# Two rows per layer norm instruction, and a float32 product as three fp32r passes, in a four-stage graph and expert network on one core

## The chip, the cores and the metric

The kernel runs on one core of one Trainium2 chip. Its five engines work side by side, each on its own queue of instructions in program order: PE (TensorE, matrix products), DVE (VectorE), ACT (ScalarE), POOL (GpSimd) and SP (SyncE, which here only issues DMAs). They are tied together by semaphores that the kernel sets and awaits itself: no scheduler moves anything. The metric is the device time of one execution in microseconds.

## The reference

There are 128 graphs of 128 nodes with 128 features. Four residual blocks follow one another, each on a layer norm of what stands before it; `_layernorm` is over the 128 features of one node:

```
def _layernorm(x, axis=-1, eps=1e-05):
    m = jnp.mean(x, axis=axis, keepdims=True)
    v = jnp.var(x, axis=axis, keepdims=True)
    return (x - m) / jnp.sqrt(v + eps)
...
    x = x + _L0_gnn_ref(_layernorm(x, axis=-1), adj, ...)       # 5 groups of nodes, two graph convolutions
    x = x + _L0_ffn_ref(_layernorm(x, axis=-1), ...)            # 8 experts, best 2 of each node
    x = x + _L1_gnn_ref(_layernorm(x, axis=-1), adj, nodemask, ...)
    x = x + _L1_ffn_ref(_layernorm(x, axis=-1), ...)            # shared MLP + 4 experts, best 2
```

The shared MLP of the last block, whose second product is changed:

```
        def _shared_mlp(x, W1, b1, W2, b2, W3, b3):
            h = jax.nn.relu(x @ W1 + b1)
            h = jax.nn.relu(h @ W2 + b2)
            return h @ W3 + b3
```

## The kernel before

All of `x` stays in the chip's memory as `xtok`: 128 partitions (the node), 128 graphs, 128 features. So the "row" of one layer norm is 128 contiguous float32 of one partition, and two graphs' rows of the same node lie 512 bytes apart. Layer norm is made of steps on several engines: DVE takes `bn_stats` of one graph (six numbers per node: for the even and for the odd features a count, a mean and a sum of squared deviations) and `bn_aggr`, which joins the two halves to mean and variance; DVE adds the epsilon (`pre`), POOL raises it to the power -1/2 (`root`), DVE makes the bias (`nb`), and ACT applies scale and bias (`xn`, `xs`, `xl`).

The program runs four stages one after another.

1. **First stage (0 to about 240 us).** Turns `t` = 0 to 27, written out. In turns 0 to 15 (`first`) one batch of grouped nodes gets its layer norm (four `bn_stats`, L650, four `bn_aggr`, L654) and starts its graph convolutions. In turns 9 to 24 (`second`) eight graphs get the result added (L645) and the statistics of the second layer norm: eight `bn_stats` (helper `stats`, L630, in groups of 2, 3, 3) and eight `bn_aggr` (helper `averages`, L635, in groups of 4 and 4), then `gpre` (L727), POOL's `groot` (L415) and `gnb` (L763). `search` finds the two best experts. Turns 9 to 15 carry `first` and `second` both.
2. **Sorting** of the nodes by expert (to about 300 us).
3. **Expert stage** (to about 817 us): 71 tiles of 512 nodes. Nothing in it is changed.
4. **Last stage (about 818 us to the end).** Four graphs are one batch; there are 32 batches and 36 turns `j`. One turn works on five batches in different phases: `complete` (batch j: gather both experts' rows, add them to `xtok`), `norm` (j-1: third layer norm), `aggregate` (j-2: graph product, then the fourth layer norm), `hidden` (j-3: the last block's first products and its router) and `finish` (j-4: the rest, and the output).

In the last stage the order on each queue is that of the code. On DVE one turn is, with the lines that matter: addition of the identity to the adjacency `at` (L1654); `stats(j-1, 0)`: four `bn_stats` of the third layer norm (L1636); `x4l` (L1663), the low part of `x4t`; `averages` of the same (L1644); the router's first step (L1669); `variance` (L1649), which lets POOL start the root; `cwd` (L1682), which waits for PE's transpose `p_ta` (L1529); bias and update (L1690 to L1702); `stats(j-2, 1)` and `averages` of the fourth layer norm (L1636, L1644), `variance` (L1649); router steps; `rc` (L1731, L1739), which PE's last products (L1553) wait for; router steps, and among them `nb[1]` (L1755), which waits for POOL's second root; the output sum `outx` (L1780); `cws` (L1786 to L1789); and `choice(0)` and `choice(1)` (L1629): the gathered rows of batch j times their probabilities added to `xtok`, four instructions each, with the copy `idx` between (L1797).

POOL has in each turn four indirect gathers, root 0, four indirect gathers, root 1, in this order (`body`, L1372 to L1390). Root 0 waits for the third layer norm's variance, root 1 for the fourth's.

Of the shared MLP, PE multiplies by `sW1` in `up(c, E1)` (L1557) as three passes in fp32r: weights and data are each split into a high part that fp32r holds and a low part, and hi x hi, lo x hi and hi x lo are summed in PSUM. The second product (L1509, in the helper `product`, L1469) takes float32 operands: `ws[:, P:2*P]` times `hs[0]`, which ACT's `relu` (L1460, at L1405) wrote at the end of the turn before. Its result is read by ACT's next `relu` into `hs[1]` (L1432).

Of the kernel before, what the change touches and what calls it, by code (L numbers as in the profile page):

```python
# [16 lines left out]
F32 = mybir.dt.float32  # L17
F16 = mybir.dt.float16
F32R = mybir.dt.float32r
# [6 lines left out]
P = 128  # L26
# [75 lines left out]
def build(nc, x_tok, x_grp, a_grp, w_grp, fus, wg, bg, w_exp, a_t, w_gcn, b_gcn, mask_t,  # L102
# [8 lines left out]
    with top:  # L111
# [90 lines left out]
        with ExitStack() as ctx:  # L202
# [19 lines left out]
            st = [alloc(ctx, f"st{p}", [P, R, 6]) for p in range(2)]  # L222
            mv = [alloc(ctx, f"mv{p}", [P, R, 2]) for p in range(2)]
# [19 lines left out]
            gst = alloc(ctx, "gst", [P, RG, 6])  # L243
            gmv = [alloc(ctx, f"gmv{p}", [P, RG, 2]) for p in range(2)]
# [72 lines left out]
            with nc.Block() as block:  # L317
# [264 lines left out]
                def _(dve):  # L582
# [30 lines left out]
                    for t in TURNS:  # L613
# [14 lines left out]
                        def stats(ks):  # L628
                            for k in ks:
                                last = nc.vector.bn_stats(gst[:, k, :], xtok[:, RG * b + k, :])  # L630
                            return last

                        def averages(ks):
                            for k in ks:
                                last = nc.vector.bn_aggr(gmv[u][:, k, :], gst[:, k, :])  # L635
                            return last
# [10 lines left out]
                        if first:  # L647
                            dve.wait_ge(loaded[p], 32 * (t // 2) + 32)
                            for k in range(R):
                                last = nc.vector.bn_stats(st[p][:, k, :], xg[p][:, k, :])  # L650
                            last.then_inc(stat_s, 1)
                            dve.wait_ge(stat_s, t + 1)
                            for k in range(R):
                                last = nc.vector.bn_aggr(mv[p][:, k, :], st[p][:, k, :])  # L654
                            last.then_inc(mv_s, 1)
                            dve.wait_ge(mv_s, t + 1)
                            nc.vector.tensor_scalar(pre[p][:, 0:R], mv[p][:, :, 1], 1e-5, None, ALU.add)
# [13 lines left out]
                        if second:  # L671
                            dve.wait_ge(x1_ready, b + 1)
                            stats(range(2))
# [3 lines left out]
                        if second:  # L677
                            stats(range(2, 5))
# [3 lines left out]
                        if second:  # L682
                            stats(range(5, RG)).then_inc(gstat_s, 1)
# [11 lines left out]
                        if first:  # L695
                            dve.wait_ge(dinv_s, 4 * t + 1)
                            dve.wait_ge(root_done, t + 1)
                            nc.vector.tensor_tensor(dinv[t % GA][:, :], nz[p][:, :], root[p][:, R:2 * R], ALU.mult)\
                              .then_inc(dinv_s, 1)
                            dve.wait_ge(dinv_s, 4 * t + 2)  # L700
                            nc.vector.tensor_tensor(dsc[p][:, :], dinv[t % GA][:, :], root[p][:, 0:R], ALU.mult)\
                              .then_inc(dinv_s, 1)
                            dve.wait_ge(dinv_s, 4 * t + 3)
                            nc.vector.scalar_tensor_tensor(xsb[p][:, :], mv[p][:, :, 0], -1.0, dsc[p][:, :],
                                                           ALU.mult, ALU.mult).then_inc(xsb_ready, 1)
                            dve.sem_inc(dinv_s, 1)
# [5 lines left out]
                        if second:  # L712
                            dve.wait_ge(gstat_s, b + 1)
                            averages(range(R))
# [3 lines left out]
                        if second:  # L718
                            averages(range(R, RG)).then_inc(gmv_s, 1)
                        if search:  # L720
                            m0 = mask[0][:, RG * c:RG * c + RG, :]
                            m1 = mask[1][:, RG * c:RG * c + RG, :]
                            after(4)
                            step(same(m0, wd, tv[2]))
                        if second:
                            dve.wait_ge(gmv_s, b + 1)
                            nc.vector.tensor_scalar(gpre[u][:, :], gmv[u][:, :, 1], 1e-5, None, ALU.add)\  # L727
                              .then_inc(gpre_ready, 1)
# [32 lines left out]
                        if second:  # L761
                            dve.wait_ge(groot_done, b + 1)
                            nc.vector.scalar_tensor_tensor(gnb[u][:, :], gmv[u][:, :, 0], -1.0, groot[u][:, :],  # L763
                                                           ALU.mult, ALU.mult).then_inc(gnb_ready, 1)
# [480 lines left out]
        with ExitStack() as ctx:  # L1245
# [15 lines left out]
            st = [alloc(ctx, f"st_l{k}", [P, R, 6]) for k in range(2)]  # L1261
            mv = [alloc(ctx, f"mv_l{k}", [P, R, 2]) for k in range(2)]
# [54 lines left out]
            x4l_ready = sem("l_x4l_ready")  # L1317
            w1_s = sem("l_w1_s")
# [18 lines left out]
            with nc.Block() as block:  # L1337
# [60 lines left out]
                def _(act):  # L1398
# [17 lines left out]
                    def body(i, p, complete, norm, aggregate, hidden, finish):  # L1416
# [42 lines left out]
                        if hidden:  # L1459
                            relu(c, 4, hs[0][:, :], bs[:, 0:1])  # L1460

# [3 lines left out]
                def _(pe):  # L1465
# [26 lines left out]
                    def body(i, p, complete, norm, aggregate, hidden, finish):  # L1492
# [74 lines left out]
                def _(dve):  # L1567
# [29 lines left out]
                    nc.vector.tensor_copy(w1h[:, 0:E1, :], w1[:, :, :])  # L1597
                    nc.vector.tensor_copy(w1h[:, E1, :], ws[:, 0:P]).then_inc(w1_s, 1)
                    dve.wait_ge(w1_s, 1)
                    nc.vector.tensor_tensor(w1l[:, 0:E1, :], w1[:, :, :], w1h[:, 0:E1, :].bitcast(F32), ALU.subtract)  # L1600
                    nc.vector.tensor_tensor(w1l[:, E1, :], ws[:, 0:P], w1h[:, E1, :].bitcast(F32), ALU.subtract)\
# [14 lines left out]
                    def body(i, p, complete, norm, aggregate, hidden, finish):  # L1616
# [18 lines left out]
                        def stats(n, k, r):  # L1635
                            ins = nc.vector.bn_stats(st[k][:, r, :], row(n, r))  # L1636
                            if r == R - 1:
                                ins.then_inc(ln[k], 1)
# [12 lines left out]

                        if norm:
# [6 lines left out]
                            for r in range(R):  # L1659
                                stats(j - 1, 0, r)  # L1660
# [4 lines left out]
                        if norm:  # L1665
                            averages(j - 1, 0)
# [20 lines left out]
                        if norm:  # L1687
# [5 lines left out]
                            nc.vector.scalar_tensor_tensor(nbm[:, :], mv[0][:, :, 0], -1.0, rd[:, :],  # L1693
# [10 lines left out]
                        if aggregate:  # L1704
                            dve.wait_ge(x3_ready, j - 1)
                            dve.sem_inc(passed, 1)
                            for r in range(R):
                                stats(b, 1, r)
# [3 lines left out]
                        if aggregate:  # L1712
                            averages(b, 1)
# [39 lines left out]
                        if aggregate:  # L1753
                            dve.wait_ge(root_done[1], j - 1)
                            nc.vector.scalar_tensor_tensor(nb[1][:, :], mv[1][:, :, 0], -1.0, root[1][:, :],  # L1755
# [117 lines left out]
```

## Time and profile before

| | us |
|---|---|
| median of 3 runs | 1334.93 (1333.78 to 1335.29) |
| the profiled execution's own time | 1336.69 |
| its span, first to last instruction | 1334.8 |
| PE busy | 1193.2 (89%) |
| DVE busy | 1137.0 (85%) |
| ACT busy | 997.9 (75%) |
| POOL busy | 843.4 (63%) |
| mean granted TensorE clock | 0.937 |

Busy times are sums of durations, and a duration of an engine that pipelines its work reaches past the start of the next instruction. So the time that an instruction costs its queue is the distance from its start to the next one's start, which the timeline view shows. Idle time in front of an instruction stands in square brackets with what ended it, if it is long enough to be listed.

### The profile page before, as it was taken

The page shows a single profiled execution, that of the slowest core. Times are in us where ns is not written, and L with a number is a line of the kernel's source. Part 1 is how long each engine was busy: PE and PEld are TensorE (multiplying, and loading weights), DVE is VectorE, ACT ScalarE, POOL GpSimd, SP SyncE. Part 2 cuts the span into 40 slices and gives each one's busy share as a digit, 9 for nine tenths or more (in the row PEclk, how much of TensorE's full clock was granted, in tenths as well). Part 3 has the DMA queues.
Part 4 walks back from the last instruction along what each step waited for, and adds up shares of the span by engine and source line. Part 5 has one row for each costly group of instructions (what it writes and reads, how often), then busy time and mean ns, then how long its engine had stood idle before and what let it go on. Part 6 is the DMA issues. An engine that isn't in the chain of part 4 may idle for free. (4 is left out here: it accounts for less than half of the span.)

```text
span 1334.8 us, 21838 instructions
## 1 busy us (share of the span) xinstructions
PE 1193.2 (89%) x6288; PEld 870.6 (65%) x6288; DVE 1137.0 (85%) x4033; ACT 997.9 (75%) x1947; POOL 843.4 (63%) x781
## 2 busy tenths in 40 slices
PE   5889988364999999999999993499999999999998
PEld 4767757253777777777777772366666666666665
DVE  4778998897899998999999996589898988989885
ACT  3457666493999999999999993477777777777774
POOL 3345555675777777777777763676666666667630
PEclk9999975576999999999999997599999999999999
DMA  5578764400222332322222262123222322222210
GB/s 183 200 234 265 210 184 137 169 1 19 69 80 78 78 78 78 80 79 80 79 78 79 77 77 62 54 62 85 65 70 69 84 67 70 76 76 68 68 48 24
DMA packets 137642, 124.89 MB, mean 94 GB/s; under 512 B 15630, under 2 KB 117106, under 8 KB 136371
## 3 DMA queue, kind: packets, MB, share of 16 engines
q1 hardware_dynamic: 119219, 88.06, 21.4%
q0 software_dynamic: 18304, 35.44, 11.8%
q8 instruction: 51, 0.84, 0.3%
q14 instruction: 68, 0.56, 0.1%
HBM read 83.78 MB, written 39.67 MB: 92 GB/s over the span
## 5 line engine op out<-in xcount | busy, mean ns | idle before, releaser
L1069 POOL DMA_INDIRECT exg<-xln_scratch,eidx x284 | 315.2, 1110 | 124.3 <-issue 69.3
L1362 POOL DMA_INDIRECT yg<-expert_rows_scratch,idx x256 | 253.4, 990 | 95.2 <-issue 72.5
L1208 DVE TENSOR_TENSOR ehl<-ehr,ehh 128x512 fp32r<-128x512 f32 x284 | 194.7, 686 | 28.7 <-ACT ehh L1093 28.5
L1090 ACT ACTIVATE ehr<-p_eh,bc 128x512 f32<-128x512 f32 x284 | 195.9, 690 | 25.1 <-PE p_eh L1128 17.0
L1093 ACT ACTIVATE ehh<-ehr 128x512 fp32r<-128x512 f32 x284 | 179.6, 633 | 9.0
L1369 POOL TENSOR_TENSOR root_l<-pre_l,mhalf 128x4 f32<-128x4 f32 x64 | 66.6, 1041 | 96.9 <-DVE pre_l L1649 96.2
L1126 PE MATMUL p_ey<-ehh,wh 128*128 128x512 f32 x284 | 124.8, 439 | 1.0 <-DVE ehl L1208 0.8
L1126 PE MATMUL p_eh<-exh,wh 128*128 128x512 f32 x284 | 124.0, 437 | 1.5 <-DVE exl L1203 1.5
L1128 PE MATMUL p_eh<-exh,wl 128*128 128x512 f32 x284 | 112.6, 396 | 0.0
L1127 PE MATMUL p_eh<-exl,wh 128*128 128x512 f32 x284 | 112.2, 395 | 0.0
L1128 PE MATMUL p_ey<-ehh,wl 128*128 128x512 f32 x284 | 111.9, 394 | 0.0
L1127 PE MATMUL p_ey<-ehl,wh 128*128 128x512 f32 x284 | 111.5, 393 | 0.0
L1405 ACT ACTIVATE he<-p_lh,be 128x512 f32<-128x512 f32 x128 | 87.8, 687 | 21.9 <-PE p_lh L1479 21.9
L1190 DVE TENSOR_TENSOR wl<-wall,wh 128x512 fp32r<-128x512 f32 x142 | 98.5, 693 | 4.9
L1629 DVE SCALAR_TENSOR_TENSOR xtok<-yg,prob,xtok 128x128 f32<-128x128 f32 x256 | 73.0, 346 | 19.3 <-DMA yg<-expert_rows_scratch,idx 16.7
L1126 PEld LDWEIGHTS p_ey<-ehh,wh 128*128 128x128 f32 x284 | 53.1, 187 | 47.6 <-DVE ehl L1208 40.7
L1475 PE MATMUL p_lh<-x4h,w1h 128*128 128x512 f32 x160 | 77.2, 483 | 1.4 <-ACT he L1405 1.3
L1411 ACT ACTIVATE xn<-xtok,nb,rd 128x128 f32<-128x128 f32 x128 | 52.8, 482 | 28.2 <-DVE nb L1702 28.1
L1553 PEld LDWEIGHTS p_out<-w,rc 128*128 128x128 f32 x512 | 59.6, 191 | 18.0 <-DVE rc L1731 17.9
L1553 PE MATMUL p_out<-w,rc 128*128 128x128 f32 x512 | 65.4, 281 | 5.1 <-DVE rc L1731 2.6
L911 PE MATMUL p_id<-hh,lc 128*128 128x284 f16 x224 | 40.5, 349 | 32.4 <-DVE hh L978 32.4
L1469 PE MATMUL p_lh<-he,w 128*64 128x512 f32 x256 | 68.8, 617 | 0.0
(228 smaller groups left out, 3152.8 us busy)
## 6 DMA issues: line engine op xcount, KB each, us to landing
expert_rows_scratch<-eyo SPq DMA_DIRECT2D x71, 256.0 KB, 2.3
xtok<-in_x_tok SPq DMA_DIRECT2D x8, 1024.0 KB, 6.8
an<-in_a_t SPq DMA_DIRECT2D x16, 512.0 KB, 4.5
xln_scratch<-xl SPq DMA_DIRECT2D x16, 512.0 KB, 4.3
at<-in_a_t SPq DMA_DIRECT2D x32, 256.0 KB, 3.0
out<-outx SPq DMA_DIRECT2D x32, 256.0 KB, 2.6
wj<-in_w_grp SPq DMA_DIRECT2D x16, 321.0 KB, 4.5
exg<-xln_scratch,eidx POOLq DMA_INDIRECT x284
```

The lines of the kernel that those rows point to most:

```text
L1069: pool.indirect_dma_start(out=xg[p][:, k, :], out_offset=None, in_=xln_d, in_offset=bass.IndirectOffsetOnAxis(ap=idx[p][:, k:k + 1], axis=0))\
L1090: nc.scalar.activation(hr[c % 2][:, :], p_h[c][:, :], ACT.Relu, bias=bc[p][:, c:c + 1])\
L1093: nc.scalar.activation(hh[:, c, :], hr[c % 2][:, :], ACT.Copy).then_inc(hh_ready, 1)
L1126: nc.tensor.matmul(dst, w_hi, a_hi, start=start, stop=False)
L1127: nc.tensor.matmul(dst, w_hi, a_lo, start=False, stop=False)
L1128: return nc.tensor.matmul(dst, w_lo, a_hi, start=False, stop=stop)
L1190: nc.vector.tensor_tensor(wl[p][:, cols], w[:, cols], wh[p][:, cols].bitcast(F32), ALU.subtract).then_inc(ready, 1)
L1208: nc.vector.tensor_tensor(hl[:, c, :], hr[c % 2][:, :], hh[:, c, :].bitcast(F32), ALU.subtract)\
L1362: pool.indirect_dma_start(out=yg[p][:, c, k, :], out_offset=None, in_=y_d, in_offset=bass.IndirectOffsetOnAxis(ap=idx[p][:, c, k:k + 1], a ...
L1405: nc.scalar.activation(dst, p_h[u % 2][:, :], ACT.Relu, bias=bias).then_inc(h_ready, 1)
L1475: nc.tensor.matmul(dst, w1h[:, e, :], x4h[:, :], start=True, stop=False)
L1553: last = nc.tensor.matmul(p_out[:, k, :], rc[u][:, k * P:(k + 1) * P], w3[:, u, :], start=False, stop=(u == 1 and k == R - 1))
```

## The change

**Statistics of two rows at once.** A new helper, `two_rows`, gives `bn_stats` two graphs' rows interleaved (feature 0 of the first, feature 0 of the second, feature 1 of the first, and so on). The instruction keeps even and odd elements apart, so each graph's count, mean and sum of squared deviations come out in three numbers. `bn_aggr` is left out everywhere, with its waits; the variance is the third number over 128, and this factor goes into the instruction that adds the epsilon. All three places use it: the two layer norms of the first stage and the two of the last.

**Three passes.** The product with `sW2` is made as `up` makes the first: weights split once into `s2h` and `s2l` at the start of the stage; each turn ACT copies `hs[0]` to `hsh` (fp32r) right after its `relu`, and DVE subtracts to get `hsl`, placed between `choice(0)` and the copy of `idx` (in the turns up to 7, and where no batch is completed, ahead of `choice(0)`).

```
+        def two_rows(dst, src):
+            return nc.vector.bn_stats(dst.rearrange("p r s -> p (r s)"), src.rearrange("p r d -> p d r"))
...
-            st = [alloc(ctx, f"st_l{k}", [P, R, 6]) for k in range(2)]
-            mv = [alloc(ctx, f"mv_l{k}", [P, R, 2]) for k in range(2)]
+            st = [alloc(ctx, f"st_l{k}", [P, R, 3]) for k in range(2)]
...
                             relu(c, 4, hs[0][:, :], bs[:, 0:1])
+                            act.wait_ge(h_ready, 8 * c + 7)
+                            nc.scalar.activation(hsh[:, :], hs[0][:, :], ACT.Copy).then_inc(hsh_ready, 1)
...
                             second(c - 1, 6, 1)
-                            product(c - 1, 7, [(p_h[1][:, :], ws[:, P:2 * P], hs[0][:, :])])
+                            pe.wait_ge(h_ready, 8 * c)
+                            pe.wait_ge(hsh_ready, c)
+                            nc.tensor.matmul(p_h[1][:, :], s2h[:, :], hsh[:, :], start=True, stop=False)
+                            nc.tensor.matmul(p_h[1][:, :], s2l[:, :], hsh[:, :], start=False, stop=False)
+                            pe.wait_ge(hsl_ready, c)
+                            nc.tensor.matmul(p_h[1][:, :], s2h[:, :], hsl[:, :], start=False, stop=True)\
+                              .then_inc(h_done, 1)
...
-                        def averages(n, k):
-                            dve.wait_ge(ln[k], 2 * n + 1)
-                            dve.sem_inc(passed, 1)
-                            for r in range(R):
-                                last = nc.vector.bn_aggr(mv[k][:, r, :], st[k][:, r, :])
+                        def stats(n, k):
+                            for r in range(0, R, 2):
+                                last = two_rows(st[k][:, r:r + 2, :], xtok[:, R * n + r:R * n + r + 2, :])
                             last.then_inc(ln[k], 1)
 
                         def variance(n, k):
-                            dve.wait_ge(ln[k], 2 * n + 2)
-                            nc.vector.tensor_scalar(pre[k][:, :], mv[k][:, :, 1], 1e-5, None, ALU.add)\
+                            dve.wait_ge(ln[k], n + 1)
+                            nc.vector.tensor_scalar(pre[k][:, :], st[k][:, :, 2], 1.0 / D, 1e-5, ALU.mult, ALU.add)\
                               .then_inc(pre_ready[k], 1)
...
+                        filling = isinstance(j, int) and j < 8
+
+                        def rest():
+                            dve.wait_ge(hsh_ready, j - 2)
+                            nc.vector.tensor_tensor(hsl[:, :], hs[0][:, :], hsh[:, :].bitcast(F32), ALU.subtract)\
+                              .then_inc(hsl_ready, 1)
+
+                        if hidden and (filling or not complete):
+                            rest()
                         if complete:
                             dve.wait_ge(gathered[p], 64 * i + 128)
                             dve.sem_inc(passed, 1)
                             for r in range(R):
                                 choice(0, r)
+                            if hidden and not filling:
+                                rest()
```

In the first stage, `second`'s eight `bn_stats` become four (in groups of 1, 1 and 2 where they were 2, 3 and 3), and `first`'s four become two. Two setup instructions on DVE make `s2h` and `s2l`.

How the order moves on DVE in a middle turn of the last stage, from `choice(0)` to the third layer norm's variance (`yg` are gathered rows, `st_l` statistics, `mv_l` mean and variance, `sm` router scores, `pre_l` variance plus epsilon). Before:

```order
L1629 SCALAR_TENSOR_TENSOR xtok<-yg,prob,xtok 128x128 x4
L1797 COPY idx<-pos_i 128x8
L1629 SCALAR_TENSOR_TENSOR xtok<-yg,prob,xtok 128x128 x4
L1654 TENSOR_TENSOR at<-at,cf 128x512
L1636 BN_STATS st_l<-xtok 128x6 x4
L1663 TENSOR_TENSOR x4l<-x4t,x4h 128x512
L1644 BN_AGGR mv_l<-st_l 128x2 x4
L1669 TENSOR_TENSOR sm<-p_llg,gbs 128x16
L1649 TENSOR_SCALAR pre_l<-mv_l 128x4
```

The same stretch of DVE's queue in the changed kernel:

```order
L1630 SCALAR_TENSOR_TENSOR xtok<-yg,prob,xtok 128x128 x4
L1783 TENSOR_TENSOR hsl<-hs,hsh 128x512
L1796 COPY idx<-pos_i 128x8
L1630 SCALAR_TENSOR_TENSOR xtok<-yg,prob,xtok 128x128 x4
L1648 TENSOR_TENSOR at<-at,cf 128x512
L151 BN_STATS st_l<-xtok 128x6 x2
L1656 TENSOR_TENSOR x4l<-x4t,x4h 128x512
L1660 TENSOR_TENSOR sm<-p_llg,gbs 128x16
L1643 TENSOR_SCALAR pre_l<-st_l 128x4
```

`hsl` (128x512) has come in, two of four `bn_stats` and all four `bn_aggr` have gone. On ACT, from the end of one turn into the next (`hs`, `rp`: results of the `relu`s; `x4t`, `x4h`: the last block's input, whole and high part; `agt`: the graph product), before:

```order
L1411 ACTIVATE xn<-xtok,nb,root_l 128x128 x4
L1405 ACTIVATE hs<-p_lh,bs 128x512
L1405 ACTIVATE rp<-p_lh,be 128x512
L1424 ACTIVATE x4t<-p_tb 128x512
L1426 ACTIVATE x4h<-x4t 128x512
L1429 ACTIVATE agt<-p_ta 128x512
```

And in the changed kernel:

```order
L1402 ACTIVATE xn<-xtok,nb,root_l 128x128 x4
L1396 ACTIVATE hs<-p_lh,bs 128x512
L1453 ACTIVATE hsh<-hs 128x512
L1396 ACTIVATE rp<-p_lh,be 128x512
L1415 ACTIVATE x4t<-p_tb 128x512
L1417 ACTIVATE x4h<-x4t 128x512
L1420 ACTIVATE agt<-p_ta 128x512
```

`hsh` stands between the `relu` that makes `hs` and all that PE awaits from ACT at the start of the next turn.

## Rows read from the trace of the kernel before

**Rows 1.** Busy time by stretch: stretch, total, busy by engine, PEclk, DMA share, GB/s.

```profile
112.00:160.00 48.00, 46.49 (x315) 37.25 (x313) 45.88 (x236) 35.25 (x76) 27.77 (x16) 0.96 0.82 247
1000.00:1100.00 100.00, 98.00 (x553) 66.03 (x553) 89.67 (x438) 76.87 (x177) 67.10 (x68) 1.00 0.27 73
```

**Rows 2.** Chain that ended last, one turn of the last stage: start us, us, what.

```profile
897.31 1.06 POOL root_l L1369
...
900.99 1.14 DVE xtok L1629 x4
902.28 1.14 DVE xtok L1629 x4
...
903.94 0.86 DVE st_l L1636 x4
...
905.31 0.37 DVE mv_l L1644 x4
905.97 1.03 POOL root_l L1369
...
912.00 1.05 POOL root_l L1369
```

**Rows 3.** Timeline of DVE, one turn: start us, us, engine, line, operation, [idle before].

```profile
1051.41 0.86 DVE L1636 BATCH_NORM_STATS2 st_l<-xtok 128x6 f32<-128x128 f32 x4
1052.19 0.67 DVE L1663 TENSOR_TENSOR x4l<-x4t,x4h 128x512 fp32r<-128x512 f32 x1
1052.78 0.37 DVE L1644 BATCH_NORM_AGGREGATE mv_l<-st_l 128x2 f32<-128x6 f32 x4
1053.07 0.14 DVE L1669 TENSOR_TENSOR sm<-p_llg,gbs 128x16 f32<-128x16 f32 x1
...
1054.38 0.68 DVE L1682 TENSOR_TENSOR cwd<-p_ta,own 32x512 fp32r<-32x512 f32 x1 [0.72 <-PE p_ta L1529]
```

**Rows 4.** Waits from 900 to 1300 us: total us, times, longest us.

```profile
POOL root_l L1369 <- DVE pre_l L1649: 74.4, 28, 7.5
...
DVE cwd L1682 <- PE p_ta L1529: 12.3, 27, 0.7
...
DVE nb L1755 <- POOL root_l L1369: 7.7, 22, 0.6
```

**Rows 5.** DVE's groups by line: count, busy us, mean ns, idle before.

```profile
L953 DVE TENSOR_TENSOR posf<-p_rank,base_r 128x512 f32<-128x512 f32 x2 | 2.2, 1079 | 0.6 <-PE p_rank L903 0.6
...
L1581 DVE TENSOR_REDUCE selp<-selraw 32x256 fp32r<-32x1024 f32 x1 | 1.9, 1873 | 0.0
...
L1583 DVE TENSOR_REDUCE own<-selraw 32x4 f32<-32x1024 f32 x1 | 1.2, 1197 | 0.0
```

**Rows 6.** Timeline of PE, the same turn.

```profile
1050.63 1.12 PE L1469 MATMUL p_lh<-hs,ws 128*128 128x512 f32 x2
1051.59 0.95 PE L1515 MATMUL p_llg<-gws,x4t 128*128 128x4 f32 x8
...
1060.89 0.47 PE L1475 MATMUL p_lh<-x4h,w1h 128*128 128x512 f32 x1
...
1061.76 1.08 PE L1469 MATMUL p_lh<-he,w 128*64 128x512 f32 x4
```

**Rows 7.** Timeline of ACT, the same turn.

```profile
1049.52 0.63 ACT L1426 ACTIVATE x4h<-x4t 128x512 fp32r<-128x512 f32 x1
...
1051.79 0.69 ACT L1405 ACTIVATE hs<-p_lh,bs 128x512 f32<-128x512 f32 x1 [0.35 <-PE p_lh L1469]
1053.66 1.15 ACT L1437 ACTIVATE gr<-p_tb,dm 128x128 f32<-128x128 f32 x4 [1.18 <-PE p_tb L1521]
```

**Rows 8.** Timeline of the first stage, an early turn.

```profile
56.22 0.95 PE L521 MATMUL p_thin<-ones,ag 128*128 128x1 f32 x8
...
57.05 0.17 DVE L657 TENSOR_SCALAR pre<-mv 128x4 f32<-128x4 f32 x1
...
57.20 0.16 DVE L659 TENSOR_SCALAR nz<-p_thin 128x4 f32<-128x4 f32 x1
```

**Rows 9.** Timeline of DVE, first stage, a late turn.

```profile
202.97 0.17 DVE L763 SCALAR_TENSOR_TENSOR gnb<-gmv,groot 128x8 f32<-128x8 f32 x1 [0.25 <-POOL groot L415]
...
207.33 0.17 DVE L727 TENSOR_SCALAR gpre<-gmv 128x8 f32<-128x8 f32 x1
...
209.33 0.17 DVE L763 SCALAR_TENSOR_TENSOR gnb<-gmv,groot 128x8 f32<-128x8 f32 x1 [0.19 <-POOL groot L415]
```

More of the change, by code:

```diff
@@ L221, in build @@
             wb = alloc(ctx, "wb", [P, NGB])
-            st = [alloc(ctx, f"st{p}", [P, R, 6]) for p in range(2)]
-            mv = [alloc(ctx, f"mv{p}", [P, R, 2]) for p in range(2)]
+            st = [alloc(ctx, f"st{p}", [P, R, 3]) for p in range(2)]
             pre = [alloc(ctx, f"pre{p}", [P, 2 * R]) for p in range(2)]
@@ L242, in build @@
             tv = [alloc(ctx, f"tv{k}", [P, RG]) for k in range(3)]
-            gst = alloc(ctx, "gst", [P, RG, 6])
-            gmv = [alloc(ctx, f"gmv{p}", [P, RG, 2]) for p in range(2)]
+            gst = [alloc(ctx, f"gst{p}", [P, RG, 3]) for p in range(2)]
             gpre = [alloc(ctx, f"gpre{p}", [P, RG]) for p in range(2)]
@@ L629, in stats @@
                             for k in ks:
[L630 to L635, printed above, removed]
+                                last = two_rows(gst[u][:, k:k + 2, :], xtok[:, RG * b + k:RG * b + k + 2, :])
                             return last
@@ L648, in _ @@
                             dve.wait_ge(loaded[p], 32 * (t // 2) + 32)
-                            for k in range(R):
-                                last = nc.vector.bn_stats(st[p][:, k, :], xg[p][:, k, :])
+                            for k in range(0, R, 2):
+                                last = two_rows(st[p][:, k:k + 2, :], xg[p][:, k:k + 2, :])
                             last.then_inc(stat_s, 1)
                             dve.wait_ge(stat_s, t + 1)
[L653 to L657, printed above, removed]
+                            nc.vector.tensor_scalar(pre[p][:, 0:R], st[p][:, :, 2], 1.0 / D, 1e-5, ALU.mult, ALU.add)
                             dve.wait_ge(deg_done, t + 1)
@@ L672, in _ @@
                             dve.wait_ge(x1_ready, b + 1)
-                            stats(range(2))
+                            stats((0,))
                         if search:
@@ L677, in _ @@
                         if second:
-                            stats(range(2, 5))
+                            stats((2,))
                         if search:
@@ L682, in _ @@
                         if second:
-                            stats(range(5, RG)).then_inc(gstat_s, 1)
+                            stats((4, 6)).then_inc(gstat_s, 1)
                         if search:
@@ L711, in _ @@
                                                     ALU.mult).then_inc(zs_ready, 1)
-                        if second:
-                            dve.wait_ge(gstat_s, b + 1)
-                            averages(range(R))
                         if search:
@@ L725, in _ @@
                         if second:
-                            dve.wait_ge(gmv_s, b + 1)
-                            nc.vector.tensor_scalar(gpre[u][:, :], gmv[u][:, :, 1], 1e-5, None, ALU.add)\
+                            dve.wait_ge(gstat_s, b + 1)
+                            nc.vector.tensor_scalar(gpre[u][:, :], gst[u][:, :, 2], 1.0 / D, 1e-5, ALU.mult, ALU.add)\
                               .then_inc(gpre_ready, 1)
@@ L762, in _ @@
                             dve.wait_ge(groot_done, b + 1)
-                            nc.vector.scalar_tensor_tensor(gnb[u][:, :], gmv[u][:, :, 0], -1.0, groot[u][:, :],
+                            nc.vector.scalar_tensor_tensor(gnb[u][:, :], gst[u][:, :, 1], -1.0, groot[u][:, :],
                                                            ALU.mult, ALU.mult).then_inc(gnb_ready, 1)
@@ L1317, in build @@
             x4l_ready = sem("l_x4l_ready")
+            s2h = alloc(ctx, "s2h", [P, P], F32R)
+            s2l = alloc(ctx, "s2l", [P, P], F32R)
+            hsh = alloc(ctx, "hsh", [P, W], F32R)
+            hsl = alloc(ctx, "hsl", [P, W], F32R)
+            hsh_ready = sem("l_hsh_ready")
+            hsl_ready = sem("l_hsl_ready")
             w1_s = sem("l_w1_s")
@@ L1597, in _ @@
                     nc.vector.tensor_copy(w1h[:, 0:E1, :], w1[:, :, :])
+                    nc.vector.tensor_copy(s2h[:, :], ws[:, P:2 * P])
                     nc.vector.tensor_copy(w1h[:, E1, :], ws[:, 0:P]).then_inc(w1_s, 1)
@@ L1600, in _ @@
                     nc.vector.tensor_tensor(w1l[:, 0:E1, :], w1[:, :, :], w1h[:, 0:E1, :].bitcast(F32), ALU.subtract)
+                    nc.vector.tensor_tensor(s2l[:, :], ws[:, P:2 * P], s2h[:, :].bitcast(F32), ALU.subtract)
                     nc.vector.tensor_tensor(w1l[:, E1, :], ws[:, 0:P], w1h[:, E1, :].bitcast(F32), ALU.subtract)\
@@ L1658, in body @@
                             dve.sem_inc(passed, 1)
-                            for r in range(R):
-                                stats(j - 1, 0, r)
+                            stats(j - 1, 0)
                         if hidden:
@@ L1706, in body @@
                             dve.sem_inc(passed, 1)
-                            for r in range(R):
-                                stats(b, 1, r)
+                            stats(b, 1)
                         if hidden:
@@ L1754, in body @@
                             dve.wait_ge(root_done[1], j - 1)
-                            nc.vector.scalar_tensor_tensor(nb[1][:, :], mv[1][:, :, 0], -1.0, root[1][:, :],
+                            nc.vector.scalar_tensor_tensor(nb[1][:, :], st[1][:, :, 1], -1.0, root[1][:, :],
                                                            ALU.mult, ALU.mult).then_inc(nb_ready[1], 1)
```

15 lines of the change are left out of this document (2 added, 13 removed).

## The prediction, before the changed kernel ran

> **What bounds the kernel now.** I read the busy time by stretch first [rows 1]. In the last stage PE looks like the bound, 98 us of 100, DVE is at 90, ACT at 77, POOL at 67. But busy time counts pipelined durations past the next start, so it does not tell which engine is waited for. The chain that ended last does [rows 2]: between 860 and 960 us it holds no PE at all. It runs in a ring of DVE and POOL: POOL's second root of a turn (897.31) lets DVE make `nb[1]`; DVE goes on without a gap through the router, the output sum, both `choice` groups, the adjacency, `bn_stats`, `x4l`, `bn_aggr` and the variance; POOL's first root (905.97) waits for that, is followed by four gathers, and only then comes the second root (912.00). Once round is 912.00 - 897.31 = 14.69 us: 8.66 from the second root to the first, 6.03 from the first to the second. The waits say the same from both ends [rows 4]: POOL waits 74.4 us for the variance in 28 waits, 2.7 us each, and DVE waits for POOL's second root in 22 turns of 27, 7.7 us in all. So what DVE does between `nb[1]` and the third layer norm's variance costs its full length, and what it does in the other half, from the variance to `nb[1]`, has slack: 0.72 us ahead of `cwd` [rows 3] and some 0.3 us ahead of `nb[1]`. PE is close behind, since it takes part in a second ring over `cwd` and `rc`.
>
> In the first stage PE and DVE are both near full from 112 to 160 us, 46.5 and 45.9 us of 48 [rows 1].
>
> **What `hsl` costs in the ring.** It is a float32 subtraction of 128x512 into fp32r, as `x4l` is: 52.19 to 52.78, 0.59 us of the queue [rows 3]. It stands between `choice(0)` and `idx`, inside the ring half that has no gap. Its whole length is paid: +0.59 us a turn. Queued behind it are `choice(1)` and the variance, for which POOL waits. It hides nowhere: POOL's later four gathers come after root 0.
>
> **What the statistics give in the ring.** Four `bn_stats` take 51.41 to 52.19, 0.78 us, and four `bn_aggr` 52.78 to 53.07, 0.29 us [rows 3]; 1.07 go. Two two-row instructions come. The trace has none, so I bound one. Below: if it took elements at the rate of a contiguous one, its queue time is that of one `bn_stats`, 0.195 us, plus 128 more elements. The rate is that of the 1024 contiguous elements of L1583, (1197 - 130) / 1024 = 1.04 ns (130 ns being about the shortest duration of DVE, that of the small L1669) [rows 3, 5]: 0.195 + 0.133 = 0.33 us. Strided: the two-row instruction reads its elements 512 bytes apart, back and forth. The nearest row is L1581, which reduces the very data of L1583, but with steps of 1024 bytes from element to element: 1873 ns where the contiguous reading takes 1197 [rows 5], (1873 - 130) / 1024 = 1.70 ns. L953 writes in steps of 32 bytes and takes 1079 ns for 512 elements, while `x4l`, as large and contiguous, takes 670 [rows 3, 5]: the same kind of price. At 1.70 ns a two-row instruction is 256 x 1.70 = 0.435, plus the 0.06 that `bn_stats` has beside its 128 elements: 0.50 us, dearer than the 0.39 of the pair that it replaces. Upper end: alternating steps at twice the contiguous time, 0.60 us; no row excludes it. I take 0.50, by L1581, and keep 0.33 and 0.60.
>
> The Trainium skill has a rule on this, in "SBUF — State Buffer", "Door 1: The DMA port swizzle": memory lines are 16 bytes, and an access that crosses to another line pays, so only strides up to four float32 are free. Every element of a two-row read crosses. By that rule, and L1581 agrees with 1.63 times the time, the change loses in the ring. The other page, "VectorE: DVE Perf Modes", "Mode 1× (REGULAR) — the baseline", says of the plain mode that odd strides all work at one result per cycle. By that, the lower end would hold, which is the first rival; L1581 speaks against it.
>
> The ring then changes by +0.59 + 2 x 0.50 - 1.07 = +0.52 us a turn (contiguous +0.18, twice +0.72). It closes in the turns that have `hidden`, a batch to complete and gathers to issue, j = 3 to 30, less one that awaits a gather anyway: 27. So +14.0 us (+4.9; +19.4).
>
> **The other half of the ring, PE and ACT.** The fourth layer norm's statistics lie between `cwd` and `rc`: 1.00 for 1.07 us, hidden in the slack. PE's product takes 50.63 to 51.59, 0.96 us; three fp32r passes took 60.89 to 61.76, 0.87 us, where the next group begins [rows 6]. That is -0.1 us a turn on an engine that the ring does not wait for: nothing. It counts in the last four turns only, with the shorter statistics, -0.5 us in all. `hsh` costs ACT as much as `x4h`, 0.63 us. ACT stands idle 0.35 us before `hs[1]` and 1.18 before `gr` in that turn, 1.53 together, both waiting for PE [rows 7], so it is absorbed; were that cover gone, PE would be late by at most 0.6. `hsl` is ready at about 1050.2, and PE wants it half a microsecond after 1050.63 at the earliest. The setup of `s2h` and `s2l` stands in DVE's queue ahead of a wait for the first gathers: nothing.
>
> **First stage.** Turns 0 to 8: the variance is ready at 57.05 + 0.17, but the step after it, L659, starts at 57.20, about when PE's sums L521 end (56.22 + 0.95 = 57.17) [rows 8]. An earlier variance gives nothing. Turns 9 to 15 (7 turns): six pairs at +0.11 are +0.66, twelve `bn_aggr` at 0.29 per four are -0.87, a semaphore wait less -0.1: -0.31 us each, on an engine that is full: -2.2 us. Turns 16 to 24: DVE's path `gnb` to `gpre` (202.97 to 207.33) and POOL's root back to `gnb` (209.33) is a ring of 6.36 us [rows 9]; four pairs +0.44, eight `bn_aggr` -0.58: -0.14 in about five turns, -0.7; the others wait for PE. Together -2.9. Contiguous: -1.33 on DVE in turns 9 to 15, of which PE's near full queue leaves about 1.0, -7, and -0.82 in five, -4: -11. Twice: +0.29 and +0.26, +3.3.
>
> **Sum.** 14.0 - 0.5 - 2.9 = +10.6 us on the profiled execution's 1336.69 (span 1334.8), so 1347.3. The median lies 1.76 below the profiled execution: 1345.5.
>
> **Rivals.**
> 1. *Two-row reads at the contiguous rate.* +4.9 - 1 - 11 = -7 us: 1328. For it: `bn_stats` works at one element per cycle, perhaps slower than its reads could come. Against: L1581 and L953 [rows 5]. It turns to the other sign when a two-row instruction costs under about 0.41 us: then the first stage gives more than the ring takes.
> 2. *The ring does not bind; PE does.* If DVE's half without gap had hidden slack, `hsl` would be free and PE's 0.1 us and its shorter waits for `rc` would show, some 0.3 us x 31 = -9, with -3 of the first stage: 1323. For it: PE at 98% [rows 1]. Against: the chain [rows 2] and 22 waits of 27 for POOL [rows 4].
> 3. *Stride at twice the contiguous time, 0.60 us.* 19.4 + 3.3 = +22.7: 1357.6.
> 4. *The gains and losses cancel*, at a cost of about 0.41 us: 1335.
>
> **How the numbers follow.** Forecast (about 0.5 us) 0.56, rival 1 0.19, rival 2 0.07, rival 3 0.10, rival 4 0.08. A measurement of this kernel tells 0.2% (2.7 us) from no change. Slower: 0.56 + 0.10, less 0.01 of the forecast's own lower tail: 0.65. Faster: 0.19 + 0.07, 0.26. Same: 0.09. The forecast's own range is 1340 to 1351; to leave out no more than 2 in 10 the range reaches down to rival 1 and up to near rival 3: 1327 to 1355. The time is 1345.5.
>
> **What would show it.** Right: a two-row `bn_stats` of about 0.58 us in duration and 0.50 between starts; a turn of 15.2 us between POOL's second roots; more idle time of PE ahead of its transposes of `xn`, as `nb[1]` comes later; `nb[1]` waiting for POOL in nearly every turn; the first stage 3 us shorter. Wrong: two-row instructions of 0.41 us with a turn near 14.87 and a first stage some 10 us shorter (rival 1), or a turn below 14.7 with PE without gaps (rival 2). Waits of PE's third pass for `hsl`, or of `rp` and `x4t` for ACT, would say that I mis-sized the covers.

## The result, and the profile after

| | before | changed |
|---|---|---|
| median, 22 runs each | 1336.33 us (1330.45 to 1340.42) | 1331.43 us (1327.55 to 1334.11) |
| span of the profiled execution | 1334.8 us | 1328.2 us |
| mean granted TensorE clock | 0.937 | 0.942 |

The ratio is 0.9964, 95% interval 0.9954 to 0.9974: 4.8 us faster (3.5 to 6.1). I had forecast 10.6 us slower, so the sign was wrong, and so was the size. The median lies inside the range from 1327 to 1355 and near rival 1 (1328).

The new instruction in the changed kernel, by tile (duration in ns: min/median/max, then first and last start):

```profile
L151 DVE BATCH_NORM_STATS2 st_l<-xtok x128: 402/419/442, 827.6 to 1299.4; 128x6 f32<-128x256 f32 x128
L151 DVE BATCH_NORM_STATS2 gst<-xtok x64: 405/422/439, 83.5 to 214.6; 128x6 f32<-128x256 f32 x64
```

It takes 0.42 us. I had expected 0.58, and 0.41 is what contiguous elements would have cost. This price, 0.50 us between starts where 0.34 was measured, is the step that failed first; a second one follows below. One turn of the changed kernel on DVE, from `nb[1]` to the third layer norm's variance, answers to [rows 3] and to the chain in [rows 2]:

```profile
1054.84 0.16 DVE L1743 SCALAR_TENSOR_TENSOR nb<-st_l,root_l 128x4 f32<-128x4 f32 x1 [0.94 <-POOL root_l L1360]
...
1058.51 0.69 DVE L1783 TENSOR_TENSOR hsl<-hs,hsh 128x512 fp32r<-128x512 f32 x1
1059.11 0.17 DVE L1796 COPY idx<-pos_i 128x8 int32<-128x8 int32 x1
1059.19 1.13 DVE L1630 SCALAR_TENSOR_TENSOR xtok<-yg,prob,xtok 128x128 f32<-128x128 f32 x4
...
1060.84 0.76 DVE L151 BATCH_NORM_STATS2 st_l<-xtok 128x6 f32<-128x256 f32 x2
1061.52 0.67 DVE L1656 TENSOR_TENSOR x4l<-x4t,x4h 128x512 fp32r<-128x512 f32 x1
1062.11 0.17 DVE L1660 TENSOR_TENSOR sm<-p_llg,gbs 128x16 f32<-128x16 f32 x1
1062.19 0.16 DVE L1643 TENSOR_SCALAR pre_l<-st_l 128x4 f32<-128x4 f32 x1
```

From `nb[1]` to the variance are 62.19 - 54.84 = 7.35 us. In the kernel before, the same half took 7.34 (60.54 to 67.88, by its next turn). `hsl` is paid in full, 0.60; the two-row statistics take 0.68 instead of 0.78, and 0.29 of `bn_aggr` are gone. The other 0.18 I had not seen: two small waits of the kernel before lay in the same half. Here they are on its DVE queue, in front of the second and the third of these rows:

```profile
1049.53 0.16 DVE L1797 COPY idx<-pos_i 128x8 int32<-128x8 int32 x1
1049.75 1.14 DVE L1629 SCALAR_TENSOR_TENSOR xtok<-yg,prob,xtok 128x128 f32<-128x128 f32 x4
...
1053.19 0.17 DVE L1649 TENSOR_SCALAR pre_l<-mv_l 128x4 f32<-128x4 f32 x1
```

`choice(1)` awaits the end of `choice(0)`, since both write `xtok`. It started 0.22 us behind `idx`, now 0.08, because `hsl` stands between and covers the wait: 0.14. And the variance came 0.12 behind the router's step [rows 3], now 0.08. Sum: 0.60 - 0.10 - 0.29 - 0.14 - 0.04 = 0.03, against 0.01 read from the starts. The middle turns of the last stage are as long as before, 14.7 us.

The waits between 900 and 1290 us, beside [rows 4]:

```profile
DVE nb L1743 <- POOL root_l L1360: 22.8, 26, 0.9
...
PEld p_lh L1504 <- ACT rp L1396: 21.1, 26, 0.8
...
DVE cwd L1673 <- PE p_ta L1528: 6.5, 27, 0.4
```

DVE now waits 0.9 us for POOL's second root in every turn, where it was 0.3: the shorter statistics of the other half fell into slack and turned into this wait, as forecast. New in the list is that the weight load of PE's first pass (PEld) waits for ACT's `rp`, which `hsh` has pushed back: 0.8 us a turn. PE itself, whose loads run beside its products, shows no idle time that ends with it.

In spans, the last stage from its first `bn_stats` on took 1334.8 - 833.4 = 501.4 us before and 1328.2 - 827.6 = 500.6 now. The rest of the profiled difference, 5.8 us, lies ahead of it.

### The profile page after: what moved, and what is told of

Read it like the earlier page. It is cut to its first block and busy times, and to the rows that moved or that the text cites. A ratio compares the mean times of both kernels' runs of the same rounds, so it can differ in the third digit from the quotient of the medians.

```text
span 1328.2 us, 21264 instructions
## 1 busy us (share of the span) xinstructions
PE 1182.5 (89%) x6320; PEld 874.2 (66%) x6320; DVE 1115.1 (84%) x3395; ACT 1014.6 (76%) x1979; POOL 846.3 (64%) x781
## 5 line engine op out<-in xcount | busy, mean ns | idle before, releaser
L1055 POOL DMA_INDIRECT exg<-xln_scratch,eidx x284 | 320.6, 1129 | 124.5 <-issue 69.5
L1353 POOL DMA_INDIRECT yg<-expert_rows_scratch,idx x256 | 257.0, 1004 | 95.7 <-issue 72.6
L1402 ACT ACTIVATE xn<-xtok,nb,root_l 128x128 f32<-128x128 f32 x128 | 52.7, 481 | 29.4 <-DVE nb L1743 29.3
L1472 PE MATMUL p_lh<-x4l,w1h 128*128 128x512 f32 x160 | 64.1, 401 | 3.4 <-DVE x4l L1656 3.4
```

What stands on the lines that cost most here:

```text
L1055: pool.indirect_dma_start(out=xg[p][:, k, :], out_offset=None, in_=xln_d, in_offset=bass.IndirectOffsetOnAxis(ap=idx[p][:, k:k + 1], axis=0))\
L1353: pool.indirect_dma_start(out=yg[p][:, c, k, :], out_offset=None, in_=y_d, in_offset=bass.IndirectOffsetOnAxis(ap=idx[p][:, c, k:k + 1], a ...
L1402: last = nc.scalar.activation(xn[k][:, r, :], xtok[:, bass.ds(R * b + r, 1), :].rearrange("p a d -> p (a d)"), ACT.Identity, scale=scale[: ...
```

## The experiments

The question after the result: is it the ring of DVE and POOL that sets the turn (ring theory), or PE's own work (PE theory)? Each part was put in alone, the ring was opened from POOL's side, and the stride was measured by itself. Ratios are to the kernel before on the same chip, with 95% intervals. "Turn" is the distance between two starts of `outx` on DVE in a middle turn.

**Statistics only** (`hsh`, `hsl`, `s2h` and `s2l` and what makes them are left out too)

```
-                            pe.wait_ge(hsh_ready, c)
-                            nc.tensor.matmul(p_h[1][:, :], s2h[:, :], hsh[:, :], start=True, stop=False)
...
+                            product(c - 1, 7, [(p_h[1][:, :], ws[:, P:2 * P], hs[0][:, :])])
```

> The changed kernel with the second product in float32 again, so without hsh and hsl: only the statistics are changed. Ring theory (DVE's half without gap and POOL's half with four gathers set the last stage's turn): four bn_stats 0.78 us become two two-row ones 0.68, 0.29 of bn_aggr and 0.04 go, -0.43 us in each of 28 turns, -12, and -6.6 of the first stage as in the changed kernel's profile: about 18 us under the kernel before, ratio 0.986, and a turn of 14.3 us. PE theory (PE's own work sets the turn, and the ring only follows it): the turn stays 14.7, the gain is the first stage's alone, -7, ratio 0.995.

Measured: 1317.18 us, ratio 0.9875 (0.9852 to 0.9897), 16.7 us under the kernel before. Two `outx` in its trace:

```profile
1107.80 0.69 DVE L1752 TENSOR_TENSOR outx<-xtok,p_out 128x512 f32<-128x512 f32 x1
1122.08 0.69 DVE L1752 TENSOR_TENSOR outx<-xtok,p_out 128x512 f32<-128x512 f32 x1
```

A turn of 14.28 us, as the ring theory had it. PE does exactly the work of the kernel before, so PE's work did not set the 14.7. But the ring is no longer alone here: PE's idle time between 900 and 1250 us is down to 1.8 us (6.1 before), and opening the ring as well, below, takes the turn only to 14.25. So this run shows that the ring set the 14.7, and not how much shorter than 14.28 it would have become.

**The three passes only**

> The kernel before with only the three fp32r passes. Ring theory: hsl adds 0.59 us and hides a semaphore wait of 0.14 us, +0.45 in 28 turns, and the filling turns lose as in the changed kernel (4 x 0.75): +13 to +16 us, ratio 1.011. PE theory: PE's product is 0.1 us shorter in 31 turns, -3 us, ratio 0.998.

Measured: 1349.43 us, ratio 1.0124 (1.0093 to 1.0155), 16.5 us slower:

```profile
1109.27 0.69 DVE L1796 TENSOR_TENSOR outx<-xtok,p_out 128x512 f32<-128x512 f32 x1
1124.39 0.69 DVE L1796 TENSOR_TENSOR outx<-xtok,p_out 128x512 f32<-128x512 f32 x1
```

A turn of 15.12 (expected 14.69 + 0.45 = 15.14). The three passes are a loss: they save PE 0.1 us where nobody waits for PE, and put 0.6 us of DVE where everybody waits for DVE. In the changed kernel the two parts all but cancel in the last stage.

**Contiguous reading**

```
-            return nc.vector.bn_stats(dst.rearrange("p r s -> p (r s)"), src.rearrange("p r d -> p d r"))
+            return nc.vector.bn_stats(dst.rearrange("p r s -> p (r s)"), src.rearrange("p r d -> p (r d)"))
```

> The changed kernel with the two-row instruction reading the same 256 elements in the order of memory, so the statistics are those of mixed rows: what is changed is only the stride. Theory that the stride is free: the instruction stays at 419 ns and the ratio at 0.996. Theory that alternating rows cost something beside the element count (my prediction had 0.50 us between starts, the profile shows about 0.34): the instruction gets shorter, and the ratio falls below 0.996.

This kernel does not compute the layer norm; only its time is of use. Measured: ratio 0.9977 (0.9962 to 0.9991), not told apart from the changed kernel's, and the instruction by tile:

```profile
L151 DVE BATCH_NORM_STATS2 st_l<-xtok x128: 398/410/430, 828.1 to 1299.5; 128x6 f32<-128x256 f32 x128
```

410 ns against 419: alternating between two rows costs 9 ns, not the 170 that I had scaled from L1581.

**Root after three gathers ("early3"), on the changed kernel**

```
-                        early = R // 2 if isinstance(j, int) and j <= 2 else R
+                        early = R // 2 if isinstance(j, int) and j <= 2 else 3
```

> The changed kernel with POOL's second root of a turn after three gathers of the four instead of after all four; the fourth gather follows it. Ring theory: the root comes 1.27 us earlier, DVE's wait of 0.9 us ahead of nb[1] goes, and the turn shrinks to what the second ring over cwd and rc or DVE's own 13.6 us allow, 14.0 to 14.3 us: 12 to 19 us under the changed kernel, ratio to before 0.983 to 0.988. PE theory: nothing but the wait moves, ratio 0.996.

Measured: 1314.06 us, ratio 0.9857 (0.9832 to 0.9882):

```profile
1105.30 0.69 DVE L1768 TENSOR_TENSOR outx<-xtok,p_out 128x512 f32<-128x512 f32 x1
1119.33 0.69 DVE L1768 TENSOR_TENSOR outx<-xtok,p_out 128x512 f32<-128x512 f32 x1
```

Turns of 14.0 to 14.2 (mean of 20: 14.12), and DVE's wait for the second root is gone from the waits. One number in POOL's order took off some 14 us more, three times what the whole change gave (0.986 against 0.996): the ring is confirmed from both sides.

**The same on the kernel before**

> The kernel before with POOL's second root after three gathers. The ring of DVE and POOL opens, but in the kernel before a second ring, of PE over cwd and rc with the longer statistics in DVE's part, closes at about 14.63 us a turn by my reading of the trace. So next to nothing: 14.6 to 14.7 us a turn, 0 to -2 us, ratio 0.998 to 1.000. If the ring of DVE and POOL alone set the turn, 0.4 us of 28 turns would go, as in the changed kernel: -12 us, ratio 0.991.

Measured: 1330.54 us, ratio 0.9972 (0.9957 to 0.9987):

```profile
1104.95 0.69 DVE L1780 TENSOR_TENSOR outx<-xtok,p_out 128x512 f32<-128x512 f32 x1
1119.53 0.69 DVE L1780 TENSOR_TENSOR outx<-xtok,p_out 128x512 f32<-128x512 f32 x1
```

The mean of 20 turns is 14.66, before 14.71, and DVE's wait for the root is gone. What sets the turn now lies less than 0.1 us below the first ring. By the expectation it is the second ring, over `cwd` and `rc`: DVE's wait ahead of `cwd` has grown from 12.3 to 20.1 us in 27 turns, which fits, but no run changes that ring alone, so its name is argued. The new statistics shorten both halves of DVE's turn, and their 0.43 us shows nearly in full; opening the first ring alone shows almost nothing.

**Statistics in the first stage alone**

> The kernel before with the new statistics in the first stage alone. Theory that the first stage gives the changed kernel its whole gain: -5 to -7 us, ratio 0.995 to 0.996. Theory that the earlier start of the last stage in the changed kernel's profile is mostly the scatter of single executions (three_only, whose first stage is the old one, starts the last stage as early): -1 to -3 us, ratio 0.998 to 0.999. By the sum of the prediction with the contiguous price it would be -11, ratio 0.992.

Measured: 1331.46 us, ratio 0.9989 (0.9972 to 1.0005): 1.5 us, not clear of zero. My -11 for this price was far too high. From 112 to 160 us the changed kernel and then this one read

```profile
112.00:160.00 48.00, 47.67 (x347) 39.17 (x345) 45.09 (x174) 38.01 (x84) 28.63 (x17) 1.00 0.83 245
112.00:160.00 48.00, 48.00 (x336) 39.46 (x336) 42.56 (x171) 36.79 (x83) 27.38 (x17) 0.96 0.83 248
```

and PE has gone from 46.5 [rows 1] to 47.7 and 48.0 of 48: little of what DVE gave was left to take. In the late turns the ring over `gnb`, `gpre` and POOL's root did get shorter, from 6.4 to 5.9 us between two starts of `gnb` (twice in this run), but the turns behind gave it back: the last seven steps, these two among them, take 48.4 us together before and 48.5 here. The start of the last stage does not tell it either: its first `bn_stats` is at 833.4 us before and 827.6 in the changed kernel, but also at 827.0 in the profile of the three passes alone, whose first stage is the old one. Single executions scatter there by as much.

**Both: statistics only, with early3**

> Statistics only (float32 product), with POOL's second root after three gathers. With the ring opened, PE's own work should set the turn, and the float32 product be seen: 14.2 us a turn against the 14.0 to 14.2 of early3 with three passes. So 0 to 3 us above early3 and about 0 to 3 us under statistics only: ratio to before 0.986 to 0.988. If the ring of DVE and POOL still set it, the 0.43 us that statistics only saves would come on top of early3: 13.7 us a turn, ratio 0.977.

Measured: 1313.47 us, ratio 0.9851 (0.9827 to 0.9876), and a turn of 14.25:

```profile
1104.54 0.69 DVE L1752 TENSOR_TENSOR outx<-xtok,p_out 128x512 f32<-128x512 f32 x1
1118.79 0.69 DVE L1752 TENSOR_TENSOR outx<-xtok,p_out 128x512 f32<-128x512 f32 x1
```

The 0.43 us did not come on top: with the ring open something else sets the turn. PE's records have 1.7 us of gaps in 350 there, the sum of all its idle times between 900 and 1250 us, against 15.2 in the changed kernel. So it is PE, or the ring through it; the runs do not tell these two apart.

**hsl always behind choice(0) ("nofill")**

```
-                        filling = isinstance(j, int) and j < 8
+                        filling = False
```

> The changed kernel with hsl always after choice(0) where a batch is completed. If the place of hsl ahead of choice(0) makes the four turns of 15.5 us, by waiting for ACT's hsh with the whole ring behind it, they fall to 14.7: 4 x 0.75 = -3 us against the changed kernel, ratio to before about 0.994. If the filling of the pipeline makes them, nothing changes: 0.996.

Measured on the changed kernel: 1327.78 us, ratio 0.9942 (0.9924 to 0.9960). The reason, from the changed kernel's early turns, and then the same turn without filling:

```profile
876.75 0.69 DVE L1768 TENSOR_TENSOR outx<-xtok,p_out 128x512 f32<-128x512 f32 x1
...
878.47 0.69 DVE L1783 TENSOR_TENSOR hsl<-hs,hsh 128x512 fp32r<-128x512 f32 x1 [0.54 <-ACT hsh L1453]
...
892.23 0.69 DVE L1768 TENSOR_TENSOR outx<-xtok,p_out 128x512 f32<-128x512 f32 x1
```

```profile
877.89 0.69 DVE L1768 TENSOR_TENSOR outx<-xtok,p_out 128x512 f32<-128x512 f32 x1
892.62 0.69 DVE L1768 TENSOR_TENSOR outx<-xtok,p_out 128x512 f32<-128x512 f32 x1
```

Ahead of `choice(0)`, `hsl` waits for ACT's copy with the ring behind it: 15.48 us a turn, four times; now 14.73. That is 3 us. The last stage from its first `bn_stats` on takes 498.1 us where it took 500.6. In whole time the two kernels are not told apart (0.9942 and 0.9964, with overlapping intervals).

**early3 with nofill**

> early3 with hsl always after choice(0) where a batch is completed, also in the turns up to 7. In early3 the four turns in which hsl stands ahead of choice(0) take 14.5 us and the next ones 14.1; in the changed kernel 15.5 and 14.7. If the place of hsl is the cause, the four fall to 14.1: -1.6 us against early3. If it is the filling of the pipeline, nothing changes.

Measured: 1311.27 us, ratio 0.9833 (0.9808 to 0.9857), the lowest median of this study. The first four turns went from 14.5 to 14.1 us, so the place of `hsl` was the cause here too. Two middle turns together take 28.23 us, 14.12 each:

```profile
1103.54 0.69 DVE L1768 TENSOR_TENSOR outx<-xtok,p_out 128x512 f32<-128x512 f32 x1
...
1131.77 0.69 DVE L1768 TENSOR_TENSOR outx<-xtok,p_out 128x512 f32<-128x512 f32 x1
```

Only with the ring opened, here and in early3, do the three passes show 0.13 us a turn against the 14.25 of the float32 product. In whole time the three kernels are not told apart (0.9833, 0.9857 and 0.9851, with overlapping intervals).

**What a stride costs**

The changed kernel with 20 more DVE instructions in the last stage's setup, two of each kind; both of a kind agreed within 0.01 us.

> The changed kernel with 20 instructions more on DVE in the setup of the last stage (two of each kind): bn_stats of 256 elements interleaved and in order, of 512 in order and with four rows interleaved; a reduction of 1024 elements in fours in order, in fours with steps of 1024 bytes (the pattern of the setup's reduction that took 1.87 us), in eights in order; a 512-element addition in order, with both inputs in steps of 512 bytes, and with output in such steps too. Theory that only reductions into many small groups are slow: the reduction in fours in order takes 1.9 us like the strided one, and the additions all take 0.69. Theory that steps between elements cost in reductions but not in bn_stats: fours in order 1.2, strided 1.9. The price of bn_stats with two rows: 0.42 either way; with four rows interleaved it should be that of 512 in order, about 0.68.

Its DVE timeline: `bn_stats` of two rows interleaved, of 256 elements in order, of 512 in order, of four rows interleaved; then reductions of 1024 in fours in order, in fours with steps of 1024 bytes; additions of 512 in order and with interleaved inputs:

```profile
813.11 0.41 DVE L1594 BATCH_NORM_STATS2 pa<-xtok 128x6 f32<-128x256 f32 x1
813.45 0.40 DVE L1595 BATCH_NORM_STATS2 pa<-xtok 128x6 f32<-128x256 f32 x1
813.77 0.66 DVE L1596 BATCH_NORM_STATS2 pa<-xtok 128x6 f32<-128x512 f32 x1
814.36 1.00 DVE L1597 BATCH_NORM_STATS2 pa<-xtok 128x6 f32<-128x512 f32 x1
815.29 1.19 DVE L1598 TENSOR_REDUCE pb<-xtok 128x256 f32<-128x1024 f32 x1
816.41 1.86 DVE L1599 TENSOR_REDUCE pc<-xtok 128x256 f32<-128x1024 f32 x1
...
819.33 0.67 DVE L1601 TENSOR_TENSOR pe_<-xtok 128x512 f32<-128x512 f32 x1
819.92 1.09 DVE L1602 TENSOR_TENSOR pf<-xtok 128x512 f32<-128x512 f32 x1
```

L1581 had been read rightly as the price of its stride: in order, the same reduction takes 1.19. But the stride alone was not what made it dear, for four rows interleaved cost `bn_stats` 1.00 and two cost nothing. I had expected four to cost no more than 512 elements in order; that was wrong.

> The changed kernel with 20 more instructions on DVE in the last stage's setup (two of each): bn_stats of 252 to 512 elements in other patterns, and two reductions. Open is why two interleaved rows read at full speed and four do not. Theory L (two lines of memory are at hand at once, so two alternating streams are free and more are not): two rows 4096 bytes apart 0.41; three rows 0.55 to 0.65; four rows of 64 columns 0.57 (1.70 ns an element); steps of 2 elements 0.41; steps of 4, 8 and 128 elements 0.57 or so, since no line is used twice there. Theory S (the cost goes by something in the four-row pattern, such as the distance of the rows): two rows 4096 bytes apart already cost 0.57, and three rows 512 bytes apart are free. A reduction over two rows of 1024 elements takes 1.2 us by L and 1.9 by S.

The second set, all `bn_stats` of 252 or 256 elements: two rows 512 bytes apart, two rows 4096 bytes apart, three rows, four rows; then one stream in steps of 2, 4, 8 and 128 elements. The last line is a reduction of 1024 elements over two rows:

```profile
814.83 0.41 DVE L1588 BATCH_NORM_STATS2 pa<-xtok 128x6 f32<-128x256 f32 x1
815.17 0.40 DVE L1589 BATCH_NORM_STATS2 pa<-xtok 128x6 f32<-128x256 f32 x1
815.50 0.42 DVE L1590 BATCH_NORM_STATS2 pa<-xtok 128x6 f32<-128x252 f32 x1
815.84 0.56 DVE L1591 BATCH_NORM_STATS2 pa<-xtok 128x6 f32<-128x256 f32 x1
816.34 0.40 DVE L1592 BATCH_NORM_STATS2 pa<-xtok 128x6 f32<-128x256 f32 x1
816.66 0.58 DVE L1593 BATCH_NORM_STATS2 pa<-xtok 128x6 f32<-128x256 f32 x1
817.17 0.59 DVE L1594 BATCH_NORM_STATS2 pa<-xtok 128x6 f32<-128x256 f32 x1
817.68 0.56 DVE L1595 BATCH_NORM_STATS2 pa<-xtok 128x6 f32<-128x256 f32 x1
818.17 1.20 DVE L1596 TENSOR_REDUCE pb<-xtok 128x512 f32<-128x1024 f32 x1
```

Up to three alternating streams are free, four are not; the reduction over two rows (1.20) costs about what the one in fours in order does (1.19). For two rows 512 and 4096 bytes apart cost the same, and the size of a large step matters little. Theory S fails on the 4096 bytes and the reduction, theory L on the three rows. What is left of L is its kind: elements are cheap when their neighbours in memory are used soon after. Its number was two, and the measured one is three. Why the limit lies between three and four is open.

## Why the prediction was wrong, point by point

- **What bounds the kernel: right.** The ring of DVE and POOL sets the last stage's turn, with the next bound less than 0.1 us below it, and PE's 98% was not the bound. Statistics only, three passes only and early3 each moved the turn as this ring has it, to within 0.02 us in the first two; that statistics only comes out so well is luck in part, since PE has nearly no idle time left there.
- **The two-row statistics: the step that failed.** "I take 0.50, by L1581", it said; 0.34 between starts is what was measured, the lower end of my bounds. Two of them cost 0.68 us a turn and not 1.00: that is 0.32 in each of 27 turns, 8.6 of the 13.5 us that the forecast had for the last stage. The error was in the choice of the nearest row. L1581 steps by 1024 bytes as the new instruction steps by 512, and I took this as the likeness. What decides is how many streams alternate: four there, two here. L953 was no nearer: it writes one stream in steps of 8 elements. The rule of the Trainium skill ("SBUF — State Buffer", "Door 1: The DMA port swizzle") promises full bandwidth to consecutive accesses on one 16-byte line and a penalty to each access that crosses to another; I let it confirm the row. The runs differ from it on both sides: two rows cross at every element and cost 0.41 us where 256 elements in order cost 0.40, and one stream in steps of four float32, which the page still counts as free, costs 0.58.
- **`hsl` in the ring: right**, 0.60 us in full. **The small waits: left out.** The prediction put at nothing 0.18 us of waits in the same half, which `hsl` covers or `bn_aggr` takes along: 4.9 us in 27 turns, the second part of the miss. With my own lower price the forecast was still +0.18 a turn; 0.03 came.
- **The filling turns: missed.** I had seen that `hsl` stands ahead of `choice(0)` there, but not that it waits for ACT with the ring behind it: +0.78 us in four turns, +3 us. A faster fill (the first `outx` is 49.1 us behind the first `bn_stats`, before 51.8) and a faster end (the last five turns take 62.5 us, before 63.6) make up for it.
- **ACT and PE: right in time.** `hsh` and the passes cost nothing while the ring is longer; the product's saving of 0.1 us showed only when the ring was open. But a wait for `rp` was named as a sign of a mis-sized cover, and it came, 0.8 us a turn at PE's weight load. It stayed without a price, for no idle time of PE ends with it.
- **The first stage: mis-sized.** For the contiguous price I had -11 us; alone it measured -1.5 (+0.7 to -3.7). PE is full in the turns that carry `first` and `second` both, and what the late turns' ring gave was lost again in the turns behind. My -2.9 at 0.50 us lies in that interval, but by too high a price.
- **The sum.** Rival 1 said 1328, the median is 1331.4: its two errors, first stage too good by 9 and last stage too bad by 5, partly cancelled. So it is luck in part that the median lies in the range and near this rival. Part stays open: -1.5 measured for the first stage and -0.8 in the profiled last stage make -2.3 us, and the medians differ by 4.9; the scatter of the first stage between executions is large enough to hide the rest, but I did not show that it does.

## What to carry to other kernels

Find the ring first: follow the chain of waits once round, note on which queue it runs without a gap, and price an added instruction by whether it stands in that half, not by how busy its engine is. Then ask both engines of the ring: moving POOL's root ahead of one gather brought the ratio of the changed kernel from 0.996 to 0.986, some 14 us, while making PE's product cheaper gave nothing. And look how far the next bound lies: in the kernel before, the same move gave 0.997 only. When no row shows an operation, take the row that is like it in what the hardware could care about, which may not be what the code shows first; where two likenesses are possible, they are two rivals with like chances.

## What the runs showed of the hardware

- Float32 reads on DVE: one stream in steps of 4, 8 or 128 elements takes 0.56 to 0.59 us for 256 elements in `bn_stats`, in steps of 1 or 2 it takes 0.40. Two or three interleaved streams are free (0.41 for 256 elements, 0.42 for 252), four cost 0.56; reductions in fours (1.86 against 1.19 for 1024 elements) and additions (1.09 against 0.67 for 512) pay for four streams too. Each was timed twice in one execution.
- Where a DVE instruction awaits the end of one just ahead of it on the same engine, some 0.14 us go; an independent instruction between them covers it. This is read from the two timelines, not measured by itself; the three passes alone fit it, with a turn of 15.12 where 14.69 + 0.59 - 0.14 = 15.14 was expected.
